# Another sharing table, a semaphore increment in every lot and small carrier instructions in a four-layer graph kernel on one core

## The chip, the cores and the metric

The kernel runs on one core of one Trainium2 chip. The metric is the device time of one execution in microseconds (us). The kernel before takes 5687.83 us, the median of three runs (5687.65 to 5688.55). The engines are named as the profile names them: PE (TensorE, with PEld for its weight loads), DVE (VectorE), ACT (ScalarE), POOL (GpSimd) and SP (SyncE, which only issues DMAs here).

## The reference

64 batches of 256 nodes with 128 features go through four layers, all in float32. Layer 0 is the costly one, because its leaky ReLU acts on every pair of nodes and each of 256 features.

```
def L0(x, W, b, a, bias):               # W = bias = adj, 256 x 256
    s1, s2 = x @ W[:, :F].T, x @ W[:, F:].T          # [B,K,256]
    pre = s1[:, :, None, :] + s2[:, None, :, :] + b  # [B,K,K,256]
    h = where(pre >= 0, pre, 0.2 * pre)
    attn = softmax(einsum('bije,e->bij', h, a) + bias)
    return sigmoid(attn @ x)
x = x + L0(relu(layernorm(x)), ...)
x = x + L1(relu(layernorm(x)), ...)   # elu, sigmoid edges times a mask, two dense layers
x = x + L2(relu(layernorm(x)), ...)   # masked attention, exp(8 tanh(QK/8/sqrt(d)))
x = x + L3(relu(layernorm(x)), ...)   # gated recurrent graph step, 5 times
```

## The kernel before

Batches are taken in pairs. The loop has 34 turns, which are written out one after the other for every engine (`run_turns`). Turn m computes the layer-0 scores of both batches of pair m (for m below 32), and beside them layers 1 and 2 of pair m-1 and layer 3 of pair m-2. Turns 0 and 1 lack a part of that, and turns 32 and 33 have only the later layers.

The layer-0 scores of a turn are cut into 128 lots, 64 for each batch of the pair. A lot is eight blocks. A block is one [128 features x 256 nodes] float32 tile `max(W, U[:, i])` (or the same through a ReLU) for one node i, written to one place of a ring with eight places. The eight blocks of every lot are shared among three engines by the table `SHARES`: the first ones go to DVE, the next to POOL and the last to ACT. DVE makes 1, 2, 4 or more neighbouring blocks with one instruction: 256 elements wide at L586, 512 or more at L591. POOL makes one block per instruction at L480, and ACT one per instruction at L779. When all three have signalled (`by_dve`, `by_pool`, `by_act`), PE multiplies the eight blocks with four 32-column matmuls (L980; the profile shows each as two matmuls and two weight loads, so a lot is 8 of them) and signals `freed`. An engine may write a place again only when the lot eight before it is freed.

The table comes from a planner, `share_blocks` (L111). It walks over the lots with one running time for each of the three engines. For every lot it takes the share whose latest end is smallest, at a fixed price per block and per lot: 2.67 per DVE block, 3.57 per ACT block, 4.5 per POOL block, and 1.0 for each lot on POOL (`POOL_START`). It adds what each engine does for the other layers in that lot (`stage_costs`). One planner unit stands for 0.1 us.

The other stages stand at fixed lots in every engine's stream (the tables `POST`, `PRE`, `LN1` to `L3`, counted in lots of a turn). An engine works its queue in order, so a stage that waits holds the blocks behind it. PE does the stages of lot t already behind lot t-3 (`LEAD`). At the turn's border these matter:

- lot 122: DVE adds the output of layer 3 (L735, `OUT`), which waits for PE's last transposes of that layer (L1127);
- lot 2: DVE computes the statistics for the norm of layer 3 (L638, then L644 `mv`), and POOL turns them into the norm's factors (L452 to L457) before its blocks of lot 3;
- lot 5: DVE reads the finished scores of the last batch (L620, `neg_score`);
- lot 10: DVE inverts the softmax sums (L625) and halves them (L628, `half_inv`, 2 elements wide).

Where a DVE stage needs the result that DVE itself just wrote, a ring piece is held back and put between (`one_piece`), to cover the latency.

Of the kernel before, what the change touches and what calls it, by code (L numbers as in the profile page):

```python
# [73 lines left out]
DVE_REST_TURNED, DVE_REST_ALL = 6, 7  # L74


VECTOR_BLOCK, VECTOR_START, SCALAR_BLOCK, POOL_BLOCK, POOL_START = 2.67, 0.69, 3.57, 4.5, 1.0
LARGEST = 3.4028234e38


# [98 lines left out]
def gnn_stack(nc, x, adj, L0_b, L0_a, L1_Wi, L1_bi, L1_We, L1_be, L1_Wn, L1_bn, L1_Wm, L1_bm, L2_q, L2_k, L2_v,  # L179
# [6 lines left out]
    class Turn:  # L186


        def __init__(self, m):
            self.m = m  # L190
            self.has_main = m < PAIRS
            self.has_post = [1 <= m <= PAIRS, self.has_main]
            self.has_l12 = 1 <= m <= PAIRS
            self.has_l3 = m >= 2
            self.pre_next = m < PAIRS - 1

        def at(self, per_turn, more):

            return per_turn * self.m + more

    def need(eng, sem, value):
        if value > 0:
            eng.wait_ge(sem, value)

    def run_turns(eng, body):
        for m in range(PAIRS + 2):
            body(Turn(m))

    with ExitStack() as ctx:
        def sb(name, shape):  # L210
# [54 lines left out]
        rstd0 = sb("rstd0", [P, NB])  # L265
        minus_mean0 = sb("minus_mean0", [P, NB])
        shift0 = sb("shift0", [P, NB])
        neg_score = sb("neg_score", [P, NB, N])
        prob = sb("prob", [P, NB, N])
        probT = sb("probT", [P, NB, N])  # L270
# [11 lines left out]
        X3_held = sb("X3_held", [P, 4, P])  # L282
        OUT = sb("OUT", [P, 4, P])
        st = sb("st", [P, 3, 4, 6])
        mv = sb("mv", [P, 3, 4, 2])
        var = sb("var", [P, 3, 4])
        rstd = sb("rstd", [P, 3, 4])
# [43 lines left out]
        by_dve = [sem(f"by_dve{n}") for n in range(RING)]  # L331
        by_act = [sem(f"by_act{n}") for n in range(RING)]
        by_pool = [sem(f"by_pool{n}") for n in range(RING)]
        freed = [sem(f"freed{n}") for n in range(RING)]

        x_loaded, pre_stats, pre_mv, pre_eps, pre_rstd = (sem(n) for n in "x_loaded pre_stats pre_mv pre_eps pre_rstd".split())
# [30 lines left out]
        def layer3_parts(turn, s):  # L367

            if turn.m <= PAIRS:
# [12 lines left out]
        @block.sync  # L385
        def _(sp):
            def load(dst, src, done=loaded_rest):
                sp.dma_start(dst, src, allow_slow_non_contiguous=True).then_inc(done, 16)


            sp.sem_inc(out_stored, 16)

            sp.dma_start(X0[:, 0], x_rows[0]).then_inc(x_loaded, 16)
            load(A[:], adj.rearrange("(r p) j -> p r j", p=P), loaded)
            load(a_col[:], L0_a.rearrange("(c p) -> p c", p=P), loaded)
            load(b0_col[:], L0_b.rearrange("(c p) -> p c", p=P), loaded)
            load(Wi[:], L1_Wi)
            load(We[:], L1_We.rearrange("(c p) o -> p (c o)", p=P))
            load(be[:], L1_be.partition_broadcast(P))
            load(Wn[:], L1_Wn.rearrange("(c p) o -> p c o", p=P))  # L400
            load(Wm[:], L1_Wm.rearrange("(c p) o -> p c o", p=P))
            load(bm_half[:], L1_bm.partition_broadcast(P))
            for n, b in enumerate((L1_bi, L1_bn, L3_w3_b, L3_w4_b, L3_w5_b, L3_u3_b, L3_u5_b)):
                load(cols[:, n:n + 1], b.rearrange("(p o) -> p o", o=1))
            load(raw2[:, 0], L2_q)
            load(raw2[:, 1], L2_k)
            load(Wv[:], L2_v)
            for n, w in enumerate((L3_w3_w, L3_w4_w, L3_w5_w)):
                load(raw3[:, n], w)
            load(rawu[:, 0], L3_u3_w)  # L410
            load(rawu[:, 1], L3_u5_w)

            def body(turn):
                for y in range(2):

                    if turn.has_main and (y == 0 or turn.pre_next):
                        need(sp, x1_ready, turn.at(2, y))
                        if turn.m == 0 and y == 0:

                            sp.wait_ge(pre_stats, 1)  # L420
                        b = turn.at(2, y + 1)
                        sp.dma_start(X0[:, 1 - y], x_rows[b]).then_inc(x_loaded, 16)
                if turn.has_l3:
                    sp.wait_ge(out_ready, turn.at(1, -1))
                    for y in range(2):
                        if turn.m == PAIRS + 1 and y == 1:

                            sp.wait_ge(out_ready, PAIRS + 1)
                        b = turn.at(2, y - 4)
                        sp.dma_start(out_rows[b], OUT[:, NB * y:NB * y + NB]).then_inc(out_stored, 16)  # L430
# [11 lines left out]
        def _(gp):  # L442
# [24 lines left out]
            def blocks(turn, t):  # L467
                y, p = divmod(t, LOTS_B)
                row, c = divmod(p, EC)
                place, rnd = t % RING, t // RING  # L470
                d, count, _ = SHARES[t]

                if p == 0:
                    gp.wait_ge(u_ready, turn.at(2, y + 1))
                    gp.wait_ge(w_ready, turn.at(2, y + 1))
                need(gp, freed[place], turn.at(ROUNDS, rnd))
                for n in range(d, d + count):
# [38 lines left out]
        def _(dve):  # L516
# [85 lines left out]
            def pre(p, y, value):  # L602

                if p == PRE[1 - y]["stats"]:
# [3 lines left out]
                    last.then_inc(pre_stats, 1)  # L608
                    one_piece()
                    dve.wait_ge(pre_stats, value)  # L610
                    for r in range(NB):
                        last = dve.bn_aggr(mv0[:, r], st0[:, r])
                    last.then_inc(pre_mv, 1)
            def post(p, y, value, lots_done):
                if p == POST[1 - y]["score"]:

                    dve.wait_ge(freed[RING - 1], lots_done)
                    need(dve, prob_ready, value - 1)
                    for r in range(NB):
                        last = dve.tensor_tensor_reduce(neg_score[:, r], S[y][:, r * N:(r + 1) * N], A[:, r], -1.0, LARGEST,  # L620
                                                        ALU.add, ALU.min, accum_out=neg_max[:, r:r + 1])
# [13 lines left out]
            def stats(t, ln, n, src, pair):  # L635
                if t == ln["stats"]:
# [3 lines left out]
                    one_piece()  # L640

                    dve.wait_ge(ln_stats[n], pair)
                    for r in range(4):
                        last = dve.bn_aggr(mv[:, n, r], st[:, n, r])  # L644
                    last.then_inc(ln_mv[n], 1)
# [536 lines left out]
```

## Time and profile before

| | us |
|---|---|
| median of three runs | 5687.83 |
| lowest and highest | 5687.65, 5688.55 |
| the profiled execution | 5687.65 |
| its span | 5685.0 |
| PE busy | 5607.0 (99%) |
| ACT busy | 5045.0 (89%) |
| DVE busy | 4978.0 (88%) |
| POOL busy | 4650.8 (82%) |

The span is the time from the first to the last instruction of the profile; the execution's own time is 2.65 us longer. PE's busy time counts matmuls from start to modelled end, and these overlap, so it can hide short stalls. The granted TensorE clock is full (2.4 GHz) through all the main turns. Times in the views are from the span's start.

### The profile page before, as it was taken

The numbers are of one execution on the slowest core, as the hardware profiler recorded it, in microseconds if no ns is written. First come the engines' busy times: TensorE is split into PE (matmuls) and PEld (weight loads), VectorE is DVE, ScalarE is ACT, GpSimd is POOL, SyncE is SP. The second block draws the span as 40 slices with busy tenths as digits, with TensorE's granted clock in tenths as the row PEclk, the third lists the DMA queues.
The fourth block names the chain that finished last, engine by engine and source line by source line (L and its number), as shares of the span: only waits on it lengthen the run. The fifth ranks groups of instructions, "written<-read, shape, count | busy, mean of one in ns | idle before, by whom it ended". The sixth has DMA issues, their size and how long they took to land.

```text
span 5685.0 us, 118726 instructions
## 1 busy us (share of the span) xinstructions
PE 5607.0 (99%) x40844; PEld 2178.3 (38%) x40844; DVE 4978.0 (88%) x8942; ACT 5045.0 (89%) x13145; POOL 4650.8 (82%) x9638
## 2 busy tenths in 40 slices
PE   8999999999999999999999999999999999999996
PEld 2333333333333333333333333333333333333334
DVE  9988988898988889888898888898898988889883
ACT  8999988899988989888998889998898988899883
POOL 8988888888888888888888888888888888888880
PEclk9999999999999999999999999999999999999999
DMA  0000000000000000000000000000000000000000
GB/s 14 5 3 6 7 7 6 3 6 7 7 6 3 7 6 7 6 3 7 6 7 7 6 3 6 7 7 6 3 7 6 7 6 3 7 6 7 7 5 6
DMA packets 44238, 34.15 MB, mean 6 GB/s; under 512 B 4736, under 2 KB 39552, under 8 KB 43648
## 3 DMA queue, kind: packets, MB, share of 16 engines
q1 hardware_dynamic: 43648, 26.56, 1.5%
q8 instruction: 336, 5.51, 0.4%
q14 instruction: 254, 2.08, 0.1%
HBM read 9.77 MB, written 8.39 MB: 3 GB/s over the span
## 4 chain that ended last, share of the span: by engine, by line
PE 83%; DVE 12%; ACT 3%; POOL 1%; issue 0%; DMA 0%; SPq 0%; POOLq 0%; DVEq 0%
PE S L980 51%; PE R L928 15%; DVE ring L591 8%; PE W L928 5%; PE S L928 4%; PE V L928 3%; PE R L1119 2%; ACT ring L779 2%; DVE ring L586 1%; PE R L1127 1%; POOL ring L480 1%; DVE half_inv L628 1%; PE S L972 1%; DVE st L638 0%; PE V L990 0%
## 5 line engine op out<-in xcount | busy, mean ns | idle before, releaser
L480 POOL TENSOR_SCALAR ring<-W,U 128x256 f32<-128x256 f32 x8928 | 4331.1, 503 | 361.1 <-PE S L980 342.7
L779 ACT ACTIVATE ring<-V,U_minus 128x256 f32<-128x256 f32 x10432 | 3969.3, 588 | 2.3 <-issue 1.1
L980 PE MATMUL S<-ring,a_window 128*32 128x512 f32 x32768 | 3699.4, 595 | 29.1 <-DVE ring L586 10.1
L591 DVE TENSOR_TENSOR ring<-U,W 128x512 f32<-128x512 f32 (+1 forms) x3840 | 3365.3, 905 | 50.4 <-ACT V L801 44.6
L980 PEld LDWEIGHTS S<-ring,a_window 128*32 128x32 f32 x32768 | 978.4, 109 | 2456.0 <-issue 2346.5
L586 DVE TENSOR_TENSOR ring<-U,W 128x256 f32<-128x256 f32 x2400 | 969.4, 408 | 0.0
L452 POOL TENSOR_TENSOR minus_mean<-mv,minus_one 128x4 f32<-128x4 f32 (+1 forms) x160 | 31.5, 197 | 571.5 <-DVE mv L644 476.4
L928 PE MATMUL R<-mT,W 128*128 128x512 f32 (+1 forms) x640 | 332.8, 602 | 2.1 <-ACT mT L887 2.1
L928 PE MATMUL R<-AT,h 128*128 128x256 f32 x1260 | 308.3, 388 | 2.8 <-ACT h L899 2.1
L717 DVE SCALAR_TENSOR_TENSOR rh<-tr,h3T 128x512 f32<-128x512 f32 (+1 forms) x165 | 123.1, 746 | 180.3 <-ACT tr L890 180.3
L887 ACT ACTIVATE mT<-R 128x512 f32<-128x512 f32 (+1 forms) x160 | 101.0, 632 | 196.5 <-PE R L928 195.0
L928 PEld LDWEIGHTS R<-AT,h 128*128 128x128 f32 x1260 | 228.9, 192 | 79.0 <-issue 50.3
L721 DVE TENSOR_TENSOR diff<-cand,h3T 128x512 f32<-128x512 f32 (+1 forms) x165 | 121.4, 736 | 134.5 <-ACT cand L896 134.5
L893 ACT ACTIVATE tz<-R,bias 128x512 f32<-128x512 f32 (+1 forms) x160 | 116.7, 729 | 75.9 <-PE R L1119 75.9
L928 PEld LDWEIGHTS R<-mT,W 128*128 128x128 f32 x640 | 111.8, 190 | 155.1 <-issue 149.6
L1119 PE MATMUL R<-mT,W 128*128 128x512 f32 (+1 forms) x320 | 165.3, 598 | 0.4 <-ACT tr L890 0.3
L928 PE MATMUL R<-rh,turned 128*128 128x512 f32 (+1 forms) x320 | 161.4, 586 | 0.2 <-DVE rh L717 0.2
L928 PE MATMUL R<-h3T,turned 128*128 128x512 f32 (+1 forms) x320 | 161.4, 586 | 0.0
L455 POOL TENSOR_TENSOR rstd<-var,minus_half 128x4 f32<-128x4 f32 (+1 forms) x160 | 142.7, 892 | 12.5
L673 DVE TENSOR_TENSOR selfT<-xhT,S 128x512 f32<-128x512 f32 x32 | 22.0, 686 | 131.6 <-PE S L928 131.6
L825 ACT ACTIVATE h<-X,shift,rstd 128x128 f32<-128x128 f32 x256 | 108.0, 531 | 32.3 <-POOL shift L457 32.3
L729 DVE SCALAR_TENSOR_TENSOR h3T<-gated,h3T 128x512 f32<-128x512 f32 (+1 forms) x165 | 126.1, 764 | 0.5
(172 smaller groups left out, 4107.9 us busy)
## 6 DMA issues: line engine op xcount, KB each, us to landing
X<-in_x SPq DMA_DIRECT2D x64, 128.0 KB, 2.1
X_held<-X SPq DMA_DIRECT2D x32, 256.0 KB, 2.3
out<-OUT SPq DMA_DIRECT2D x64, 128.0 KB, 1.9
raw<-in_L_gnn_w_w SPq DMA_DIRECT2D x3, 128.0 KB, 2.2
A<-in_adj SPq DMA_DIRECT2D x1, 256.0 KB, 2.6
Wn<-in_L_gnn_Wn SPq DMA_DIRECT2D x1, 128.0 KB, 2.5
Wm<-in_L_gnn_Wm SPq DMA_DIRECT2D x1, 128.0 KB, 2.4
rawu<-in_L_gnn_u_w SPq DMA_DIRECT2D x2, 64.0 KB, 2.2
```

Of the source, the lines that this page charges most:

```text
L455: gp.tensor_tensor(rstd_, eps_var, minus_half[:, 0:width], ALU.pow).then_inc(sem_rstd, 1)
L480: last = gp.tensor_scalar(ring[:, place, g, half * N:(half + 1) * N], W[:, y, c], LARGEST, U[:, y, c, i:i + 1], ALU.min, ALU.max)
L586: piece = dve.tensor_tensor(ring[:, place, g, half * N:(half + 1) * N], U[:, y, c, i:i + 1].to_broadcast([P, N]), w, ALU.max)
L591: piece = dve.tensor_tensor(ring[:, place, g:g + groups].rearrange("p g (h j) -> p g h j", h=NB), u.unsqueeze(3).to_broadcast([P, groups, ...
L717: dve.scalar_tensor_tensor(rh[:, cols_], tr[:, cols_], 1.0, h3T[:, cols_], ALU.add, ALU.mult).then_inc(rh_ready, 1)
L721: dve.tensor_tensor(diff[:, cols_], cand[:, cols_], h3T[:, cols_], ALU.subtract).then_inc(diff_ready, 1)
L729: dve.scalar_tensor_tensor(h3T[:, cols_], gated[:, cols_], 0.5, h3T[:, cols_], ALU.mult, ALU.add).then_inc(state_ready, 1)
L779: last = act.activation(ring[:, place, g, half * N:(half + 1) * N], W_scalar[y][:, c * N:(c + 1) * N], ACT.Relu, bias=U_minus[:, y, c, i:i ...
L893: act.activation(tz[:, cols_], gates[:, cols_], ACT.Tanh, bias=bias3[:, 0:1], scale=0.5).then_inc(tz_ready, 1)
L928: return pe.matmul(dst, lhsT, rhs, start=start, stop=stop)
L980: last = pe.matmul(S[y][g * ROWS:(g + 1) * ROWS, :], a_window[:, c, ROWS - 1 - row:2 * ROWS - 1 - row], ring[:, place, g], start=False, st ...
L1119: pe.matmul(gates[:, cols_], W345[:, 0], mT[:, cols_], start=False, stop=True, skip_group_check=True).then_inc(z_psum, 1)
```

## The change

`POOL_START` goes from 1.0 to 2.2, which gives another table `SHARES`. Summed over a turn the shares are 419 DVE, 279 POOL and 326 ACT blocks before, and 435, 253 and 336 after; 65 of the 128 lots have another share. DVE's pieces were 75 of one block, 68 of two and 52 of four. They are 69, 66 and 57, and one of six.

POOL increments a semaphore `pool_begun` at the start of every lot, between the wait for `freed` and the first block; nothing waits for it. DVE gets a memset of one element per partition (`wait_carrier` or `score_carrier`) behind the wait in three places: before the mean and variance are put together for layer 0 and for the norms of layers 1 to 3, and before the scores are read. `Turn` and its helpers learn a second form with a loop register `it`, but `run_turns` still makes every turn with m, so the code for that form produces nothing.

```
-VECTOR_BLOCK, VECTOR_START, SCALAR_BLOCK, POOL_BLOCK, POOL_START = 2.67, 0.69, 3.57, 4.5, 1.0
+VECTOR_BLOCK, VECTOR_START, SCALAR_BLOCK, POOL_BLOCK, POOL_START = 2.67, 0.69, 3.57, 4.5, 2.2
...
-            body(Turn(m))
+            body(Turn(m=m))
...
+        score_carrier = sb("score_carrier", [P, 1])
...
+        wait_carrier = sb("wait_carrier", [P, 1])
...
+        pool_begun = sem("pool_begun")
...
                 need(gp, freed[place], turn.at(ROUNDS, rnd))
+                gp.sem_inc(pool_begun, 1)
                 for n in range(d, d + count):
...
                     one_piece()
                     dve.wait_ge(pre_stats, value)
+                    dve.memset(wait_carrier[:], 0.0)
                     for r in range(NB):
                         last = dve.bn_aggr(mv0[:, r], st0[:, r])
...
                     need(dve, prob_ready, value - 1)
+                    dve.memset(score_carrier[:], 0.0)
                     for r in range(NB):
                         last = dve.tensor_tensor_reduce(neg_score[:, r], ...)
...
                     dve.wait_ge(ln_stats[n], pair)
+                    dve.memset(wait_carrier[:], 0.0)
                     for r in range(4):
                         last = dve.bn_aggr(mv[:, n, r], st[:, n, r])
```

DVE's queue before, from the output of layer 3 (lot 122) to the statistics of lot 2; `freedN` is the wait for the ring place of a lot, so freed6 is lot 126 and freed2 lot 2:

```order
L735 TENSOR_TENSOR OUT<-R,X_held 128x512 [waits out_stored,state_psum]
L591 TENSOR_TENSOR ring<-U,W 128x1024 [waits freed3]
L591 TENSOR_TENSOR ring<-U,W 128x512 [waits freed4]
L586 TENSOR_TENSOR ring<-U,W 128x256
L591 TENSOR_TENSOR ring<-U,W 128x1024 [waits freed5]
L591 TENSOR_TENSOR ring<-U,W 128x1024 [waits freed6]
L591 TENSOR_TENSOR ring<-U,W 128x1024 [waits freed7]
```

And the same piece of the queue now:

```order
L746 TENSOR_TENSOR OUT<-R,X_held 128x512 [waits out_stored,state_psum]
L599 TENSOR_TENSOR ring<-U,W 128x1024 [waits freed3]
L599 TENSOR_TENSOR ring<-U,W 128x512 [waits freed4]
L594 TENSOR_TENSOR ring<-U,W 128x256
L599 TENSOR_TENSOR ring<-U,W 128x1024 [waits freed5]
L599 TENSOR_TENSOR ring<-U,W 128x1024 [waits freed6]
L594 TENSOR_TENSOR ring<-U,W 128x256
L599 TENSOR_TENSOR ring<-U,W 128x1024 [waits freed7]
```

Lot 126 has one block more, an instruction of 256.

DVE's queue before from the statistics of lot 2 to lot 7:

```order
L638 BN_STATS st<-X_held 128x6 x3
L586 TENSOR_TENSOR ring<-U,W 128x256
L644 BN_AGGR mv<-st 128x2 [waits ln3_stats]
L644 BN_AGGR mv<-st 128x2 x3
L591 TENSOR_TENSOR ring<-U,W 128x512 [waits freed3]
L591 TENSOR_TENSOR ring<-U,W 128x1024 [waits freed4]
L591 TENSOR_TENSOR ring<-U,W 128x1024 [waits freed5]
L620 ISA neg_score,neg_max<-S,A 128x256 [waits prob_ready,freed7]
...
L591 TENSOR_TENSOR ring<-U,W 128x512 [waits freed6]
L591 TENSOR_TENSOR ring<-U,W 128x1024 [waits freed7]
L586 TENSOR_TENSOR ring<-U,W 128x256
```

And now:

```order
L648 BN_STATS st<-X_held 128x6 x3
L599 TENSOR_TENSOR ring<-U,W 128x512
L653 MEMSET wait_carrier 128x1 [waits ln3_stats]
L655 BN_AGGR mv<-st 128x2 x4
L599 TENSOR_TENSOR ring<-U,W 128x512 [waits freed3]
L599 TENSOR_TENSOR ring<-U,W 128x1024 [waits freed4]
L599 TENSOR_TENSOR ring<-U,W 128x512 [waits freed5]
L594 TENSOR_TENSOR ring<-U,W 128x256
L628 MEMSET score_carrier 128x1 [waits prob_ready,freed7]
...
L599 TENSOR_TENSOR ring<-U,W 128x1024 [waits freed6]
L599 TENSOR_TENSOR ring<-U,W 128x1024 [waits freed7]
```

The piece held back at lot 2 grows from one block to two, lot 5 goes from four blocks to three, lot 6 from two to four, lot 7 from five to four, and the two memsets carry the waits. DVE's queue from lot 8 to `half_inv` is unchanged.

POOL's queue before from the norm's factors to lot 8 (freed0):

```order
L457 TENSOR_TENSOR shift<-minus_mean,rstd 128x4 [waits ln3_rstd]
L480 TENSOR_SCALAR ring<-W,U 128x256 [waits freed3]
L480 TENSOR_SCALAR ring<-W,U 128x256 [waits freed4]
L480 TENSOR_SCALAR ring<-W,U 128x256 [waits freed5]
L480 TENSOR_SCALAR ring<-W,U 128x256 [waits freed6]
L480 TENSOR_SCALAR ring<-W,U 128x256 x3
L480 TENSOR_SCALAR ring<-W,U 128x256 [waits freed7]
L480 TENSOR_SCALAR ring<-W,U 128x256
L480 TENSOR_SCALAR ring<-W,U 128x256 [waits freed0]
L480 TENSOR_SCALAR ring<-W,U 128x256
```

And now (semaphore increments are not in these rows; one stands ahead of each row with a `freed` wait):

```order
L464 TENSOR_TENSOR shift<-minus_mean,rstd 128x4 [waits ln3_rstd]
L488 TENSOR_SCALAR ring<-W,U 128x256 [waits freed3]
L488 TENSOR_SCALAR ring<-W,U 128x256 [waits freed4]
L488 TENSOR_SCALAR ring<-W,U 128x256 [waits freed5]
L488 TENSOR_SCALAR ring<-W,U 128x256 [waits freed6]
L488 TENSOR_SCALAR ring<-W,U 128x256 x2
L488 TENSOR_SCALAR ring<-W,U 128x256 [waits freed7]
L488 TENSOR_SCALAR ring<-W,U 128x256 x2
L488 TENSOR_SCALAR ring<-W,U 128x256 [waits freed0]
```

Lot 6 has three blocks instead of four, lot 7 three instead of two, lot 8 one instead of two. Through lot 6 that is 6 blocks instead of 7, through lot 7 it is 9 as before.

## Rows read from the trace of the kernel before

**Rows 1.** Stretches turn 0, 1, 7: length, PE, PEld, DVE, ACT, POOL busy us, clock.

```profile
15.45:154.06 138.61, 130.19 (x1079) 36.55 (x1079) 135.70 (x230) 130.77 (x358) 131.05 (x291) 0.99 0.01 2
154.06:298.98 144.92, 141.69 (x1161) 49.35 (x1160) 137.33 (x257) 140.58 (x381) 136.72 (x298) 1.00 0.02 5
1174.19:1349.08 174.89, 174.44 (x1275) 67.46 (x1274) 155.35 (x279) 157.34 (x411) 145.84 (x301) 1.00 0.02 6
```

**Rows 2.** Chain of waits over a turn's border: start us, us, what.

```profile
1164.05 0.45 PE R L1127 x4
...
1164.52 0.69 DVE OUT L735
1165.21 1.73 DVE ring L591 x2
1166.94 0.33 DVE ring L586
...
1174.34 0.37 DVE mv L644 x4
...
1182.36 0.60 DVE ring L591
...
1183.35 1.52 DVE half_inv L628
...
1185.84 1.07 PE S L980 x8
```

**Rows 3.** The same chain, one turn later.

```profile
1339.42 0.69 DVE OUT L735
```

**Rows 4.** PE's weight loads in time, lots 2 to 11: start, us, what, [idle before].

```profile
1175.94 0.13 PEld L980 LDWEIGHTS S<-ring,a_window 128*32 128x32 f32 x4 [0.30 <-issue]
1177.09 0.19 PEld L980 LDWEIGHTS S<-ring,a_window 128*32 128x32 f32 x8 [1.02 <-issue]
...
1178.83 0.16 PEld L980 LDWEIGHTS S<-ring,a_window 128*32 128x32 f32 x4 [0.27 <-issue]
1179.81 0.19 PEld L980 LDWEIGHTS S<-ring,a_window 128*32 128x32 f32 x8 [0.81 <-issue]
1180.71 0.19 PEld L980 LDWEIGHTS S<-ring,a_window 128*32 128x32 f32 x8 [0.72 <-DVE ring L586]
...
1185.84 0.16 PEld L980 LDWEIGHTS S<-ring,a_window 128*32 128x32 f32 x8 [1.21 <-DVE ring L586]
```

**Rows 5.** POOL in order of time from the border, norm factors and lots 3 onwards.

```profile
1174.80 0.20 POOL L452 TENSOR_TENSOR minus_mean<-mv,minus_one 128x4 f32<-128x4 f32 x1 [3.95 <-DVE mv L644]
...
1176.50 10.89 POOL L480 TENSOR_SCALAR ring<-W,U 128x256 f32<-128x256 f32 x24
```

**Rows 6.** Chain of waits in turn 0, its two longest pieces.

```profile
68.61 11.66 ACT ring L779 x32
...
81.37 46.74 POOL ring L480 x103
```

**Rows 7.** Who waited for whom on POOL in turn 7: total, times, longest.

```profile
POOL minus_mean L452 <- DVE mv L644: 13.8, 3, 6.9
POOL ring L480 <- PE S L980: 11.2, 9, 3.6
```

**Rows 8.** One memset on DVE: minimum/median/maximum ns.

```profile
L739 DVE MEMSET minus_one<- x1: 62/62/62, 0.8 to 0.8; 128x4 f32 x1
```

**Rows 9.** POOL in order of time, norm factors of layer 1.

```profile
1195.74 1.02 POOL L455 TENSOR_TENSOR rstd<-var,minus_half 128x4 f32<-128x4 f32 x1
1196.83 0.20 POOL L457 TENSOR_TENSOR shift<-minus_mean,rstd 128x4 f32<-128x4 f32 x1
```

**Rows 10.** `half_inv` over the run: minimum/median/maximum ns.

```profile
L628 DVE TENSOR_SCALAR half_inv<-inv_sum x64: 156/164/1611, 96.2 to 5546.8; 128x2 f32<-128x2 f32 x64
```

**Rows 11.** DVE, then POOL, around one `half_inv` in order of time.

```profile
1183.27 1.60 DVE L628 TENSOR_SCALAR half_inv<-inv_sum 128x2 f32<-128x2 f32 x1
1181.92 4.11 POOL L480 TENSOR_SCALAR ring<-W,U 128x256 f32<-128x256 f32 x9
```

More of the change, by code:

```diff
@@ L74 @@
 DVE_REST_TURNED, DVE_REST_ALL = 6, 7
-VECTOR_BLOCK, VECTOR_START, SCALAR_BLOCK, POOL_BLOCK, POOL_START = 2.67, 0.69, 3.57, 4.5, 1.0
+VECTOR_BLOCK, VECTOR_START, SCALAR_BLOCK, POOL_BLOCK, POOL_START = 2.67, 0.69, 3.57, 4.5, 2.2
 LARGEST = 3.4028234e38
@@ L186, in gnn_stack, with __init__ @@
     class Turn:
[L189 to L195, printed above, removed]
+        def __init__(self, m=None, it=None):
+            self.m, self.it = m, it
+            self.has_main = it is not None or m < PAIRS
+            self.has_post = [it is not None or 1 <= m <= PAIRS, self.has_main]
+            self.has_l12 = it is not None or 1 <= m <= PAIRS
+            self.has_l3 = it is not None or m >= 2
+            self.pre_next = it is not None or m < PAIRS - 1
         def at(self, per_turn, more):
-            return per_turn * self.m + more
+            if self.it is None:
+                return per_turn * self.m + more
+            return self.it * per_turn + (2 * per_turn + more)
     def need(eng, sem, value):
-        if value > 0:
-            eng.wait_ge(sem, value)
+        if isinstance(value, int) and value <= 0:
+            return
+        eng.wait_ge(sem, value)
     def run_turns(eng, body):
         for m in range(PAIRS + 2):
-            body(Turn(m))
+            body(Turn(m=m))
     with ExitStack() as ctx:
@@ L267, in gnn_stack @@
         shift0 = sb("shift0", [P, NB])
+        score_carrier = sb("score_carrier", [P, 1])
         neg_score = sb("neg_score", [P, NB, N])
@@ L284, in gnn_stack @@
         st = sb("st", [P, 3, 4, 6])
+        wait_carrier = sb("wait_carrier", [P, 1])
         mv = sb("mv", [P, 3, 4, 2])
@@ L333, in gnn_stack @@
         by_pool = [sem(f"by_pool{n}") for n in range(RING)]
+        pool_begun = sem("pool_begun")
         freed = [sem(f"freed{n}") for n in range(RING)]
@@ L367, in layer3_parts @@
         def layer3_parts(turn, s):
-            if turn.m <= PAIRS:
+            if turn.it is not None or turn.m <= PAIRS:
                 return [(slice(0, 2 * N), slice(0, 2 * NB), R0, R1, turn.at(STEPS, s + 1 - 2 * STEPS),
@@ L421, in body @@
                         b = turn.at(2, y + 1)
-                        sp.dma_start(X0[:, 1 - y], x_rows[b]).then_inc(x_loaded, 16)
+                        sp.dma_start(X0[:, 1 - y], x_rows[b] if isinstance(b, int) else x_rows[bass.ds(b, 1)].rearrange("o p r d -> (o p) r d")).then_inc(x_loaded, 16)
                 if turn.has_l3:
@@ L429, in body @@
                         b = turn.at(2, y - 4)
-                        sp.dma_start(out_rows[b], OUT[:, NB * y:NB * y + NB]).then_inc(out_stored, 16)
+                        dst = out_rows[b] if isinstance(b, int) else out_rows[bass.ds(b, 1)].rearrange("o p r d -> (o p) r d")
+                        sp.dma_start(dst, OUT[:, NB * y:NB * y + NB]).then_inc(out_stored, 16)
                 if turn.has_l12:
@@ L476, in blocks @@
                 need(gp, freed[place], turn.at(ROUNDS, rnd))
+                gp.sem_inc(pool_begun, 1)
                 for n in range(d, d + count):
@@ L610, in pre @@
                     dve.wait_ge(pre_stats, value)
+                    dve.memset(wait_carrier[:], 0.0)
                     for r in range(NB):
@@ L618, in post @@
                     need(dve, prob_ready, value - 1)
+                    dve.memset(score_carrier[:], 0.0)
                     for r in range(NB):
@@ L642, in stats @@
                     dve.wait_ge(ln_stats[n], pair)
+                    dve.memset(wait_carrier[:], 0.0)
                     for r in range(4):
```

## The prediction

> **What bounds the kernel now.** I began with the busy times by stretch. In a full turn PE is busy for 174.44 of 174.89 us [rows 1], but that time counts to modelled ends, so I asked next for the chain of waits. From one turn's border to the next it is PE work without a break, except for one stretch: when PE has finished the last transposes of layer 3, DVE adds the output at 1164.52 and then runs 21.3 us without a pause, through the rest of the turn and into the next one, until its blocks of lot 11 let PE start that lot at 1185.84 [rows 2]. One turn later the same addition stands at 1339.42 [rows 3], so a turn takes 174.90 us. A turn is thus PE's work from lot 11 to lot 117, plus this DVE stretch.
>
> PE's weight loads show how much PE loses there [rows 4]. At full pace a load row and the idle ahead of it make 0.43 us (0.13 + 0.30, or 0.16 + 0.27) for half a lot. The idle ahead of lot 3 is 1.02 instead of 0.30, ahead of lot 6 it is 0.81 instead of 0.27, ahead of lot 11 it is 1.21 instead of 0.30: 0.72 + 0.54 + 0.91 = 2.17 us lost. Lot 7 comes 0.90 behind lot 6 where 0.86 is the pace, 0.04 lost. Who ends last? POOL waits for DVE's mv, makes the norm's factors and starts its blocks of lot 3 at 1176.50, then 24 without a gap at 10.89/24 = 0.454 each [rows 5]. Its first block ends near 1176.97, its seventh (the last of lot 6) near 1179.70 and its ninth (the last of lot 7) near 1180.60; PE starts lots 3, 6 and 7 each 0.11 to 0.12 us later. So these three wait for POOL, and lot 11 waits for DVE. About 2.2 us in 174.9 is all that a better sharing could win in a full turn.
>
> The two first turns are different: turn 0 (138.61 us) has DVE busy for 135.70, turn 1 (144.92 us) has ACT busy for 140.58 [rows 1], and a long piece of turn 0's chain is POOL [rows 6].
>
> **The change part by part.** Prices: a DVE piece of one block takes 0.33 us of the chain and one of two 0.60; a four and a two together take 1.73, so a four 1.13 [rows 2]. A POOL block takes 46.74/103 = 0.454 us and an ACT block 11.66/32 = 0.364 us [rows 6].
>
> Per turn the table takes 26 blocks off POOL (-11.8 us), gives ten to ACT (+3.6 us) and sixteen to DVE. In pieces DVE has six ones and two twos fewer, five fours more and one six (1.13 + 0.53 = 1.66, the step from two to four once more): -1.98 - 1.20 + 5.65 + 1.66 = +4.1 us. In a full turn most of this lies beside PE's work: of 174.89 us DVE is idle 19.5 and ACT 17.6 [rows 1]. POOL's relief is worth little there: POOL waits 11.2 us a turn for free ring places and 13.8 for DVE's mv as it is [rows 7].
>
> What counts is what falls into the DVE stretch. Lot 126: four blocks become five, +0.33. Lot 2: a held piece of one becomes one of two, +0.27. Lot 5: 1.13 becomes 0.60 + 0.33, -0.20. Lot 6: 0.60 becomes 1.13, +0.53. Lot 7: 1.13 + 0.33 becomes 1.13, -0.33. The sum is +0.60 us, all of it ahead of mv and 0 behind it.
>
> The memsets: the two in the stretch (lots 2 and 5) take 62 ns each from start to end [rows 8], and instructions overlap in that queue, so 0 to 0.06 us each. I take 0.03 each, +0.06. The others of a turn lie in covered places.
>
> The semaphore increment on POOL has no row of its own. From below: POOL's 24 blocks behind the border and its 103 in turn 0 follow at 0.454 us across lots, although each lot starts with a semaphore wait [rows 5, 6]; a semaphore operation whose condition is met costs this queue nothing, so the lower end is 0. From above: where POOL has to wait for the end of its own last instruction, the next starts 0.07 us behind it (1195.74 + 1.02 to 1196.83) instead of overlapping it by 0.02 [rows 9], so a full drain in each lot would be about 0.1 us. I take 0, the nearer row, and keep 0.1.
>
> The last term is a stall. `half_inv` handles 2 elements and takes 164 ns at the median, but up to 1611 [rows 10], and at the border it is the long form: 1.60 us [rows 11], 1.52 of them on the chain [rows 2]. In that time POOL ran on without a gap, nine blocks in 4.11 us [rows 11]: DVE was passed by three of them. That is 1.44 us for an unlucky moment. DVE comes to it over the same sum of pieces behind mv as before plus one memset, and POOL's grid of 0.454 us starts at mv too. So DVE comes about 0.03 us later against that grid. If it misses the unlucky moment, the wait is at most the rest of one block, 0 to 0.45 us, and 1.0 to 1.44 us are won; I take a wait of 0.3, 1.14 won. If it does not, nothing is won.
>
> The Trainium skill (SBUF — State Buffer, "Who interferes with whom") says of a DVE instruction in a two-port mode beside GpSimd: "Whoever issues first gets the shared pair for the whole instruction; the other **fully blocks**". The rows agree that DVE is held up while POOL runs, and disagree on how long: by the rule it would be one block, not three. By the rule alone at most 0.45 us could be won here, the border would change by 0.60 + 0.06 - 0.45 = +0.21, and the time would be 5696 us.
>
> Now the two paths to lot 11. DVE's end moves by +0.60 + 0.06 - 1.14 = -0.48 us. On PE's own path, mv and POOL's factors behind it come +0.63 later (0.60 and one memset). Through lot 7 POOL has nine blocks as before, so lot 7 starts +0.63 later, and from there PE has 0.91 us of stall to use up before lot 11: +0.63 - 0.91 = -0.28. The later of the two sets the turn, -0.28 us. What is late next is POOL at lots 3 to 7, not DVE. About 30 borders: -8.4 us.
>
> Turn 0: DVE's 135.70 + 4.1 + 7 x 0.03 = 140.0 is over the turn's 138.61, +1.4. Turn 1: ACT's 140.58 + 3.6 = 144.2 is just under 144.92; with imperfect packing I take +1 (-0.7 to +3.6). In the tail a few memsets stand on the chain, +0.1. Sum: -8.4 + 1.4 + 1.0 + 0.1 = -5.9. The profiled execution took 5687.65 us, 0.2 below the median, so 5681.8 against it and 5682 beside the median.
>
> **The rivals.**
>
> 1. *The stall stays.* DVE comes again just when POOL starts a block, since both count from mv and only a memset lies between. Then the whole +0.66 counts: 30 x 0.66 + 2.5 = +22.3, 5710 us. For it: the long form stands at the same place in a turn, so the phase is locked, and a shift of some ns may not leave it. Against it: half of the 64 `half_inv` are short although POOL is nearly always busy, so the window is narrow. It decides once the wait stays over some 0.8 us.
>
> 2. *The increment costs POOL 0.1 us a lot.* Five increments lie between mv and lot 7, +0.5: lot 11 at +0.22. 30 x 0.22 + 2.5 = +9.1, 5697 us. For it: nothing but that the price is not shown. The Trainium skill (PSUM — Partial Sum Buffer, "Engine vs sequencer instructions") counts semaphore operations as the sequencer's own, which waits only until earlier instructions are dispatched; by that the cost is 0, and no row here shows an increment of POOL's.
>
> 3. *POOL becomes the bound.* 128 increments must outweigh the 11.8 us taken off and the 11.2 us of waits for ring places, which they do from 0.18 us each. At 0.25 us it would be 32 - 23 = +9 us a turn, 5960 us. Nothing in the rows speaks for it.
>
> 4. *The relief pays where POOL is the chain.* In turn 0 some sixteen blocks leave the POOL-bound half, -7.2 us. If DVE and ACT take theirs in gaps, turns 0 and 1 get 3 us shorter each, and with -0.4 a border the sum is -18, 5670 us. Against it: DVE's busy time in turn 0.
>
> **How the numbers follow.** Forecast 0.45, rival 1 0.23, rival 2 0.14, rival 3 0.04, rival 4 0.14. A measurement of this kernel tells about 0.2% (11.4 us) from no change, so the borders are 5676.4 and 5699.2. Faster: rival 4 and a little of the forecast, 0.19. Same: most of the forecast and more than half of rival 2, 0.47. Slower: rivals 1 and 3 and the rest, 0.34. The range runs from rival 4 to rival 1 with its unknowns, 5669 to 5713; the forecast's own is 5674 to 5692.
>
> **What would show it.** A turn (one output addition to the next) should be 174.6 us. `half_inv` at the border should be under 0.65 us; if it is 1.6, rival 1 holds. PE should lose nearly nothing ahead of lot 11 and more ahead of lots 3 and 7. POOL's blocks should follow at 0.45 us across lots; a longer step is rival 2 or 3. DVE's output addition should still wait for PE. I am wrong if PE stalls elsewhere in the turn, at the updates of layer 3 (lots 29, 51, 73, 95, 117), where the added ACT and DVE blocks would then have used up the cover, or if a full turn changes by over 1 us either way.

## The result, and the profile after

The changed kernel takes 5739.15 us (median of six runs, 5728.78 to 5753.63) beside 5688.19 us for the kernel before (six runs, 5687.65 to 5688.97). The ratio is 1.009, with a 95% interval of 1.0077 to 1.0104. That is 51 us slower. The forecast was 5682 us and its range ended at 5713, so it was wrong, and not narrowly. The runs of the changed kernel also lie 25 us apart, where those of the kernel before lie 1.3 us apart. The profiled execution took 5721.63 us, less than any of the six timed ones. What it shows is therefore the lower end of the loss, and the rest has to be found by experiment. One run of the first experiment below took 11388 us, twice the time of its others, at a granted clock of 0.94, and is left out of its median.

The profile page, part 1 (busy us, share of the span, instructions): POOL's busy time fell as the table says, and DVE and ACT took it over.

```profile
PE 5615.9 (98%) x40844; PEld 2184.3 (38%) x40844; DVE 5103.7 (89%) x9102; ACT 5157.0 (90%) x13465; POOL 4247.0 (74%) x8806
```

Stretches of turn 0, turn 1 and turn 7, with the columns of [rows 1]:

```profile
15.47:155.22 139.75, 130.15 (x1078) 36.29 (x1078) 139.45 (x229) 134.21 (x369) 121.73 (x269) 0.99 0.01 2
155.22:303.19 147.97, 142.84 (x1161) 48.07 (x1160) 143.44 (x256) 144.33 (x391) 122.06 (x267) 1.00 0.02 5
1181.34:1356.84 175.50, 174.45 (x1278) 67.62 (x1274) 159.13 (x284) 160.85 (x421) 133.04 (x275) 1.00 0.02 6
```

Turn 0 lost 1.15 us, turn 1 lost 3.05, and an ordinary full turn 0.61. DVE is now busy for 139.45 of the 139.75 us of turn 0, but that counts time in which it is held up. Each batch ends with one DVE instruction that adds layer 0's output (`X<-tanh,X`, 256 elements). All executions of it, minimum/median/maximum ns, before and after:

```profile
L632 DVE SCALAR_TENSOR_TENSOR X<-tanh,X x64: 407/424/733, 104.0 to 5550.8; 128x256 f32<-128x256 f32 x64
L642 DVE SCALAR_TENSOR_TENSOR X<-tanh,X x64: 405/424/2442, 107.2 to 5581.9; 128x256 f32<-128x256 f32 x64
```

The long one stands in turn 1, while POOL runs without a gap (below: DVE, then POOL), and one of 1567 ns in turn 0 (733 before):

```profile
251.90 2.44 DVE L642 SCALAR_TENSOR_TENSOR X<-tanh,X 128x256 f32<-128x256 f32 x1
249.79 6.62 POOL L488 TENSOR_SCALAR ring<-W,U 128x256 f32<-128x256 f32 x14
```

The chain of waits over the same border (start us, us, what) answers to [rows 2, 3]:

```profile
1171.29 0.69 DVE OUT L746
...
1181.81 0.28 DVE mv L655 x3
...
1190.73 1.51 DVE half_inv L638
...
1193.22 1.07 PE S L991 x8
...
1346.79 0.69 DVE OUT L746
```

From the output addition to PE's start of lot 11 it is 21.93 us, against 21.32 before, and from one addition to the next 175.50. `half_inv` still holds the chain for 1.51 us.

PE's weight loads of lots 2 to 11 in order of time (start, us, what, idle before) answer to [rows 4]:

```profile
1184.46 0.19 PEld L991 LDWEIGHTS S<-ring,a_window 128*32 128x32 f32 x8 [1.63 <-issue]
...
1186.73 0.15 PEld L991 LDWEIGHTS S<-ring,a_window 128*32 128x32 f32 x4 [0.36 <-DVE ring L599]
1187.07 0.16 PEld L991 LDWEIGHTS S<-ring,a_window 128*32 128x32 f32 x4 [0.18 <-issue]
1188.09 0.19 PEld L991 LDWEIGHTS S<-ring,a_window 128*32 128x32 f32 x8 [0.86 <-DVE ring L599]
...
1193.22 0.16 PEld L991 LDWEIGHTS S<-ring,a_window 128*32 128x32 f32 x8 [1.21 <-DVE ring L594]
```

The idle ahead of lot 3 grew from 1.02 to 1.63 us, because mv and POOL's factors come 0.61 later. The rows of lots 6 and 7 (1186.73 and 1188.09) name DVE as the one that ended the idle time, but POOL's last block came later there: at 1187.97 for lot 7, against 1187.68 for DVE's. The idle ahead of lot 11 is 1.21 as before. Nothing was given back there.

POOL and DVE at that place, in order of time:

```profile
1183.88 11.33 POOL L488 TENSOR_SCALAR ring<-W,U 128x256 f32<-128x256 f32 x25
```

```profile
1190.65 1.59 DVE L638 TENSOR_SCALAR half_inv<-inv_sum 128x2 f32<-128x2 f32 x1
```

POOL's blocks follow at 11.33/25 = 0.453 us across some fourteen lots, with an increment in each: the increment costs POOL nothing.

What no row of before had shown are single long waits. `diff` is the first DVE instruction of each state update of layer 3 (five a turn; the first is due at lot 29). All executions of it in the trace, minimum/median/maximum ns, of the kernel after:

```profile
L732 DVE TENSOR_TENSOR diff<-cand,h3T x165: 416/693/4317, 336.5 to 5715.1; 128x512 f32<-128x512 f32 x155, 128x256 f32<-128x256 f32 x10
```

and of the kernel before:

```profile
L721 DVE TENSOR_TENSOR diff<-cand,h3T x165: 415/692/1018, 331.9 to 5680.2; 128x512 f32<-128x512 f32 x155, 128x256 f32<-128x256 f32 x10
```

The longest stands in turn 22. DVE, POOL and PE there, in order of time:

```profile
3847.09 4.32 DVE L732 TENSOR_TENSOR diff<-cand,h3T 128x512 f32<-128x512 f32 x1 [0.21 <-ACT cand L907]
3851.33 0.41 DVE L594 TENSOR_TENSOR ring<-U,W 128x256 f32<-128x256 f32 x1
```

```profile
3845.24 8.34 POOL L488 TENSOR_SCALAR ring<-W,U 128x256 f32<-128x256 f32 x15
```

```profile
3844.97 4.90 PE L991 MATMUL S<-ring,a_window 128*32 128x512 f32 x44
3852.75 1.08 PE L991 MATMUL S<-ring,a_window 128*32 128x512 f32 x4 [2.87 <-DVE ring L594]
```

DVE stands for 4.32 us over an instruction that needs 0.69 when nothing disturbs it, while POOL runs block after block. The next DVE block comes only then, and PE waits 2.87 us for it. The windows behind it show what follows (length, busy us of PE, PEld, DVE, ACT, POOL, granted clock, DMA share, GB/s):

```profile
3840.00:3852.00 12.00, 9.88 (x80) 3.01 (x72) 11.79 (x14) 12.00 (x33) 12.00 (x23) 1.00 0.01 2
3852.00:3859.00 7.00, 6.25 (x22) 1.99 (x26) 7.00 (x13) 4.45 (x12) 3.84 (x7) 0.51 0.00 0
```

PE had stood still for 2.87 us, and then the granted clock was 0.51, the lower level (1.2 GHz), for 7 us. This turn took 181.53 us (+6.03); turn 28, with a `diff` of 3890 ns and no drop of the clock, took 178.14 (+2.64).

So the 34.8 us between the two profiled spans (5685.0 and 5719.8) are: 28 ordinary turns at 0.605 = 16.9; the long waits of turns 22 and 28, and 0.25 in turn 20, 8.9; turns 0 and 1 4.2; the stretch from the last main turn's start to the end 4.6; 0.2 is left over. The term of 4.6 goes with the clock: from that start on, 40.2 us ran at the lower level in this trace, 30.9 before. Whether it is the change's own isn't settled. In the ten traces with new shares in all or part of the table the same stretch is 0.8 to 5.6 us longer than before, and roughly the longer, the more of it ran at the lower level (31.1 us for the 0.8, 43.7 for the 5.6). In the two further traces with the old table (increments and memsets alone, and no halving) it is 0.3 and 0.5 us shorter. One trace of each kernel can't tell more.

### The profile page after: what moved, and what is told of

Read it like the earlier page. It is cut to its first block, busy times and chain, and to the rows that moved or that the text cites. A ratio compares the mean times of both kernels' runs of the same rounds, so it can differ in the third digit from the quotient of the medians.

```text
span 5719.8 us, 122469 instructions
## 1 busy us (share of the span) xinstructions
PE 5615.9 (98%) x40844; PEld 2184.3 (38%) x40844; DVE 5103.7 (89%) x9102; ACT 5157.0 (90%) x13465; POOL 4247.0 (74%) x8806
## 3 DMA queue, kind: packets, MB, share of 16 engines
q14 instruction: 283, 2.32, 0.1%
## 4 chain that ended last, share of the span: by engine, by line
PE 82%; DVE 14%; ACT 2%; issue 1%; POOL 0%; DMA 0%; SPq 0%; POOLq 0%; DVEq 0%
PE S L991 50%; PE R L939 15%; DVE ring L599 10%; PE W L939 5%; PE S L939 4%; PE V L939 3%; PE R L1130 2%; DVE ring L594 2%; ACT ring L790 1%; PE R L1138 1%; DVE half_inv L638 1%; PE S L983 1%; DVE st L648 0%; PE V L1001 0%; DVE OUT L746 0%
## 5 line engine op out<-in xcount | busy, mean ns | idle before, releaser
L488 POOL TENSOR_SCALAR ring<-W,U 128x256 f32<-128x256 f32 x8096 | 3914.7, 503 | 575.0 <-PE S L991 530.7
L790 ACT ACTIVATE ring<-V,U_minus 128x256 f32<-128x256 f32 x10752 | 4100.5, 607 | 2.4 <-issue 1.2
L599 DVE TENSOR_TENSOR ring<-U,W 128x512 f32<-128x512 f32 (+1 forms) x3968 | 3555.4, 928 | 34.5 <-ACT V L812 28.8
L594 DVE TENSOR_TENSOR ring<-U,W 128x256 f32<-128x256 f32 x2208 | 894.0, 408 | 0.0
L901 ACT ACTIVATE tr<-R,bias 128x512 f32<-128x512 f32 (+1 forms) x160 | 116.5, 728 | 5.3 <-PE R L939 5.3
L907 ACT ACTIVATE cand<-R,bias 128x512 f32<-128x512 f32 (+1 forms) x160 | 118.7, 742 | 1.4 <-PE R L939 1.4
```

Of the source, the lines that this page charges most:

```text
L594: piece = dve.tensor_tensor(ring[:, place, g, half * N:(half + 1) * N], U[:, y, c, i:i + 1].to_broadcast([P, N]), w, ALU.max)
L599: piece = dve.tensor_tensor(ring[:, place, g:g + groups].rearrange("p g (h j) -> p g h j", h=NB), u.unsqueeze(3).to_broadcast([P, groups, ...
L790: last = act.activation(ring[:, place, g, half * N:(half + 1) * N], W_scalar[y][:, c * N:(c + 1) * N], ACT.Relu, bias=U_minus[:, y, c, i:i ...
L907: act.activation(cand[:, cols_], messages[:, cols_], ACT.Tanh, bias=bias3[:, 2:3]).then_inc(cand_ready, 1)
```

## Experiments

Two theories stood after this. S: the steady loss is DVE's added 0.60 us ahead of mv with the stall of `half_inv` unchanged, and the scatter is a second thing, long waits of DVE behind POOL at lot 29. R, the rival: the increments and memsets make the loss.

**The table alone.**

```
-                gp.sem_inc(pool_begun, 1)
-                    dve.memset(wait_carrier[:], 0.0)      (both)
-                    dve.memset(score_carrier[:], 0.0)
```

> The new sharing table alone: no increment on POOL, no memsets. Theory A (the table is the cause: +0.60 us of DVE blocks in the stretch at each turn's border with the long halving still in it, and new collisions of DVE with POOL's stream at lot 29): a turn of about 175.45 us, the halving at the border 1.6 us, the time 5715 to 5745 us and scattered by over 10 us. Theory B (the increment or the memsets cost the time, by slowing or shifting POOL): within 0.2% of before, 5680 to 5698 us.

Measured: 5711.55 us (three runs, 5710.93 to 5714.27), ratio 1.0043 [1.0026, 1.006]. Turns 140.13, 148.65, then 175.49 without exception. The longest `diff` took 998 ns. The table alone costs 24 us, steadily. In the profile (24.8 us) that is 28 turns at 0.60 = 16.8, turns 0 and 1 = 5.3, and 2.7 in the tail, where the clock varies. In turns 0 and 1 `X<-tanh,X` took 2004 and 2884 ns here: DVE's long waits in these two turns need neither increments nor memsets.

**The increments and memsets alone.**

```
-... POOL_START = 2.67, 0.69, 3.57, 4.5, 2.2
+... POOL_START = 2.67, 0.69, 3.57, 4.5, 1.0
```

> Increments on POOL and memsets on DVE with the sharing table of before. Theory A: 174.9 to 175.0 us a turn (two memsets of some 0.03 us at the border), 5687 to 5692 us, POOL's blocks still 0.45 us apart across lots. Theory B: most of the loss is here, 5715 us or more.

Measured: 5688.89 us (5687.33 to 5691.18, ten runs), ratio 1.0002 [0.9992, 1.0011], turns of 174.90. With the old table they cost nothing. R is refuted as it stands.

**No halving, in the kernel before and in the changed one.** ACT's copy of the probabilities halves them, and the tanh scales with `inv_sum`:

```
-  act.activation(probT[:], ..., ACT.Copy)
+  act.activation(probT[:], ..., ACT.Copy, scale=0.5)
...
-  dve.tensor_scalar(half_inv[:], inv_sum[:], 0.5, None, ALU.mult).then_inc(half_inv_ready, 1)
```

> The kernel before, but the halving of the inverse sums is folded into ACT's copy of the transposed weights (scale 0.5), so the DVE instruction that takes 1.6 us at the border is gone. If that wait is real time on the path: DVE reaches lot 11 1.5 us earlier, PE is then held by POOL at lots 3 to 7 as before and saves the 0.91 us ahead of lot 11: a turn of 174.0 us, 5658 to 5664 us. If the wait only stands in for one that the next DVE instruction would take over, or POOL's stream decides: 5685 us or more.

> The changed kernel without the halving. Theory A: the border loses the stall too, and PE is held by POOL at lots 3 to 7, which start 0.6 us later than before: 174.9 - 0.3 = 174.6 us a turn instead of 175.5, and the scatter stays if the waits of DVE at lot 29 stay, 5690 to 5720 us. If the loss of the change were not at the border, the halving's removal would give under 5 us against the changed kernel, 5730 us or more.

Measured on the kernel before: 5673.77 us (5671.78 to 5675.75), ratio 0.9974 [0.9964, 0.9983], turns of 174.38. Measured on the changed kernel: 5698.88 us (5696.06 to 5701.27), ratio to before 1.0019 [1.001, 1.0029], turns of 174.99. The whole stall is thus worth 0.51 us a turn, not 0.91. And between these two kernels, which have no stall to win or lose, the change still costs 174.99 - 174.38 = 0.61. The chain at the border of the first (start us, us, what) shows why there is nothing left to win:

```profile
1162.69 0.69 DVE OUT L733
...
1174.49 0.20 POOL shift L457
1174.69 0.46 POOL ring L480
...
1175.28 4.69 PE S L978 x40
```

The chain now leaves DVE at mv, goes over POOL's factors to lot 3, and PE runs on from there. Both paths, through lot 3 and through lot 11, contain the stretch from the output addition to mv, and that is where the +0.60 lies. In the changed kernel the removal brought 40 us on the median, far over 29 x 0.5: the scatter was gone too, and the longest `diff` took 1004 ns.

**The new shares only at the border, and only elsewhere.**

```
+SHARES = [NEW_SHARES[t] if t >= 122 or t <= 12 else OLD_SHARES[t] for t in range(LOTS)]
```

> The changed kernel with the new shares in lots 122 to 127 and 0 to 12 alone; in all other lots the old ones. Theory (the steady loss of 0.61 us a turn is DVE's 0.60 us more between the output addition and lot 11; the long waits of the state update at lot 29 and the loss in turns 0 and 1 come from the shares elsewhere): a full turn 175.5 us, no turn longer than 175.7, 30 x 0.6 = 18 on 5688, so 5704 to 5709 us, with a scatter of some 3 us between runs. Rival (the long waits come with the memsets and increments or with any longer turn): turns of 178 to 182 us here and there, 5715 to 5750 us with a scatter over 10 us.

> The changed kernel with the old shares in lots 122 to 127 and 0 to 12 and the new ones in lots 13 to 121. Theory (as above): a full turn 174.9 us apart from the turns with a long wait at lot 29, 2 to 6 us each; turn 0 and turn 1 longer by some 3 us together; 5692 to 5725 us with a scatter of over 5 us. Rival (the added DVE and ACT blocks of lots 13 to 28 cost nothing by themselves): 5688 to 5691 us without scatter.

Measured, border only: 5710.46 us (5709.04 to 5711.73), ratio 1.0039 [1.0024, 1.0054], full turns of 175.49 or 175.50 without exception, longest `diff` 1097 ns. Elsewhere only: 5709.36 us (5702.62 to 5718.09), ratio 1.0038 [1.0023, 1.0053], full turns of 174.90 except nine: 177.22, 179.14 and seven of 176.77, each with a `diff` of 3.4 to 3.9 us at lot 29. The loss has two separate halves in two separate places of the table, as S says. What S put down to the shares elsewhere alone, the loss of turns 0 and 1, comes from both: they lose +1.0 and +1.1 with the first, +0.7 and +1.7 with the second.

**A later `half_inv`.** A memset of 64, then of 512 elements of its own ahead of it:

```
                     dve.wait_ge(inv_ready, value)
+                    dve.memset(late[:], 0.0)
```

> The changed kernel with one memset of 64 elements of its own ahead of half_inv, so that DVE asks for it some 0.1 us later (a memset of one element takes 59 ns). Theory A (the long form is a matter of phase: DVE must ask while POOL starts a block): the wait falls to 0.45 us or less, and the turn to 175.0 to 175.2 us as when half_inv is gone (174.99), 5715 us or below. Theory B (whenever POOL streams without a gap, DVE is passed by three blocks there): half_inv stays at 1.5 to 1.7 us and the turn is 175.5 to 175.6 us.

> The changed kernel with a memset of 512 elements ahead of half_inv, so that DVE asks for it some 0.5 us later, one POOL block later. In the traces so far the wait ended at the 19th POOL block behind mv in nearly every turn, whether DVE asked at once or 0.08 us later. Theory C (something at that block of POOL's stream lets DVE in): half_inv shortens by what it comes later, to 1.0 to 1.2 us, the border stays at 21.9 us. Theory B (DVE is passed by three blocks wherever it asks): half_inv stays at 1.4 to 1.6 us, and the turn grows by some 0.5 us to 176.0.

Measured with 64 elements: 5738.29 us (5731.45 to 5747.75), ratio 1.0089 [1.0074, 1.0104]; ordinary turns 175.49, `half_inv` 1.52 us. With 512 elements, a single run: 5713.5 us, turns of 175.54. DVE at the border in that kernel:

```profile
1191.51 0.48 DVE L639 MEMSET late<- 128x512 f32 x1
1191.92 1.09 DVE L640 TENSOR_SCALAR half_inv<-inv_sum 128x2 f32<-128x2 f32 x1
1192.92 0.68 DVE L600 TENSOR_TENSOR ring<-U,W 128x512 f32<-128x512 f32 x1
```

Theory A, mine from the prediction, is refuted: DVE asked at two other moments and won nothing either time. Theory B (always three blocks) is refuted as well: the wait shrank by the 0.5 us that DVE came later, as theory C of the last expectation says. In the kernels before, after, table alone and both of these, `half_inv` ended 0.23 to 0.24 us into the 19th POOL block behind mv in nearly every turn. DVE's way out of the stall is thus fixed to POOL's stream, and POOL's stream is fixed to mv. Work put between mv and `half_inv` (at least up to 0.5 us) is nearly free (+0.05 us a turn for 512 elements), work put ahead of mv is paid in full. Why it is that block isn't settled.

**Which part brings the long waits at lot 29.** The new table with the increments but no memsets, then with the memsets but no increments:

```
-                    dve.memset(wait_carrier[:], 0.0)      (first kernel, all three memsets)
-                gp.sem_inc(pool_begun, 1)                 (second kernel)
```

> The changed kernel without the memsets: new table and increments. With the table alone the runs stood at 5713 us without scatter; with all three parts at 5729 to 5754 us. Theory I (the increment at the head of each lot of POOL's shifts POOL against DVE and lets the long waits of the state update at lot 29 appear): 5725 to 5750 us, scatter over 10 us, single turns of 178 to 182 us. Theory M (the memsets shift DVE against POOL): 5711 to 5715 us, every full turn 175.5 us.

> The changed kernel without the increments: new table and memsets. Theory M: 5725 to 5750 us, scatter over 10 us, single turns of 178 to 182 us. Theory I: 5711 to 5716 us, every full turn 175.5 us. If both this kernel and the one without memsets scatter, each shift alone is enough; if neither does, it takes both.

Measured without memsets: 5711.13 us (5707.68 to 5714.37), ratio 1.0041 [1.0026, 1.0056], turns of 175.49, longest `diff` 993 ns. Without increments: 5716.79 us (5712.91 to 5734.98), ratio 1.0057 [1.0041, 1.0074], two turns of 178.13 with a `diff` of 3878 ns. One of them, in turn 3:

```profile
512.78 3.88 DVE L731 TENSOR_TENSOR diff<-cand,h3T 128x512 f32<-128x512 f32 x1 [0.21 <-ACT cand L906]
```

So the memsets are what lets the waits at lot 29 in, given the new table. Which of the three memsets does it wasn't tried. With the increments on top the median is 22 us higher still (5739 and 5717), so these seem to make the waits more frequent, though alone they bring none. This second point is weaker than the first: it rests on four runs and seven, one of the four stands at 5734.98 among the seven, and both profiles have two long waits.

**The old shares in lots 13 to 29 alone.**

```
+SHARES = [NEW_SHARES[t] if not 13 <= t <= 29 else OLD_SHARES[t] for t in range(LOTS)]
```

> The changed kernel with the old shares in lots 13 to 29 alone. There the new table gives DVE one block more and ACT two more and POOL three less; DVE's blocks of lot 29 are ready 0.05 us ahead of PE with it (1.16 us in the kernel before). Theory (the long waits and the scatter come from those lots): a full turn 175.5 us with no long wait of the state update at lot 29, 5705 to 5714 us, scatter of 5 us or less. Rival (they come with the sharing behind lot 29, which sets how long POOL streams without a gap): long waits remain, 5720 to 5750 us.

Measured: 5708.98 us (5706.72 to 5709.67, five runs), ratio 1.0035 [1.0021, 1.0049]; turns of 175.50, longest `diff` 982 ns. Memsets and increments are in, the shares of 111 lots are new, and the scatter is down to 3 us. Seventeen lots decide it.

What these lots change is when DVE asks. I took the start of `diff` at lot 29 in every full turn and the start of POOL's block in hand:

| kernel | `diff` starts so far into POOL's block | and takes |
|---|---|---|
| before | 321 to 328 ns | about 706 ns |
| increments and memsets alone | 307 to 330 | about 701 |
| border only | 303 to 377 | about 697; 1097 (at 377) |
| old shares in lots 13 to 29 | 317 to 337 | about 695 |
| lighter border, no halving (below) | 211 to 222 | about 797 |
| table alone | 21 to 47 | 990, at most 998 |
| table and increments | 21 to 44 | 984, at most 993 |
| changed, no halving | 5 to 35 | 1000, at most 1004 |
| before, no halving | 26 to 56 | 976, at most 990 |
| changed, 512 elements ahead of `half_inv` | 0 to 19, once 452 | 1009, at most 1019 |
| table and memsets | 19 to 47 | 992; twice 3878 (both at 47) |
| changed | 18 to 46 | 990; 3890 (at 29), 4317 (at 46) |
| changed, 64 elements ahead of `half_inv` | 14 to 46 | 994; six times 3878 to 3886 (at 19, 28 and four times 46) |
| new shares but at the border | 15 to 37 | 991; 3885 (at 23), 3881 (at 32), eight times 3439 (at 16 or 17) |

At 0.32 us into a block DVE isn't held up, at 0.21 it is by 0.1 us. Within the first 0.05 us it always waits for the rest of that block (990 ns), and sometimes for six to eight blocks, the one in hand included. All twenty long waits of `diff` in these traces came within 16 to 47 ns of a block's start. An early request is thus what these lots bring, but not enough by itself: five kernels with it had no long wait in their profiles. What picks the turn stays open; in the changed kernel two executions at the same 46 ns, in turns 22 and 23, went both ways. No run moved the request at lot 29 by itself, with the shares left as they are.

**A lighter border.** On the kernel before, without halving:

```
+for _t, _s in ((124, (2, 3, 3)), (126, (3, 4, 1)), (127, (2, 4, 2)), (0, (2, 3, 3)), (1, (2, 4, 2))):
+    SHARES[_t] = _s
```

> The kernel before, without half_inv (ACT's copy of the probabilities halves them) and with other shares in five lots ahead of mv (DVE, POOL, ACT): lot 124 (3,2,3) to (2,3,3), 126 (4,3,1) to (3,4,1), 127 and 1 (4,2,2) to (2,4,2), 0 (3,2,3) to (2,3,3). DVE gets 0.33 + 0.20 + 0.53 + 0.33 + 0.53 = 1.9 us less ahead of mv, POOL seven blocks = 3.2 us more where it waits 3.95 us for mv [rows 5]. Theory (DVE's stretch ahead of mv sets the turn, POOL's wait there is free): the turn falls from 174.4 (half_inv removed alone) by up to what PE still loses at lots 3 to 11, to 172.9 to 173.6 us, and the time to 5625 to 5650 us. Rival (POOL comes late to mv or to lot 3, or DVE's move shifts it against POOL into a long wait elsewhere): the turn stays at 174.4 or rises, 5674 us or more.

Measured: 5660.15 us (5658.69 to 5660.52), ratio 0.995 [0.9934, 0.9967]; turns of 173.84. The mechanism is as expected, the size isn't: the turn was to be 172.9 to 173.6. I had summed the idle of PE's weight loads at lots 3 to 7 (0.72 + 0.54 + 0.04) and got 0.54, and turns 0 and 1 gave nothing (+0.5 and +0.1). The chain at the border (start us, us, what):

```profile
1160.40 0.44 PE R L1127 x4
1160.83 8.72 PE S L980 x80
1169.55 1.06 PE S L972 x2
1170.61 7.00 PE S L980 x64
1177.61 0.59 PE V L1007 x4
```

DVE is gone from it. PE runs through the border, and this is the fastest of all versions, 28 us below the kernel before. The time missed the expected 5625 to 5650 us.

## Why the prediction was wrong

**Step by step.** *The two paths at the border*: right. OUT to lot 11 through DVE, and mv to lot 3 through POOL. *The table adds 0.60 us ahead of mv*: right; the stretch grew by 0.61, and so did the turn in each pair of kernels that differ in the border's shares alone. *Memsets 0.03 each in the stretch*: too much; with the old table the turn went from 174.89 to 174.90. *The increment costs POOL nothing*: right, and rival 2 is out. POOL's pace is 0.453 us, and the kernel with increments and memsets on the old table stands at 1.0002. *Rival 3*: out by POOL's pace. *Rival 4*: out; turns 0 and 1 became longer, not shorter.

**The step that failed** is the stall: "DVE comes about 0.03 us later against that grid. If it misses the unlucky moment, the wait is at most the rest of one block ... I take a wait of 0.3, 1.14 won." The wait isn't a matter of a moment. It ends at a fixed block of POOL's stream, wherever DVE asks within half a microsecond, and the trace of before already had the hint: the long form stood at 1.60 us at the same place in every full turn, to within some ns. A chance event doesn't repeat to 1%. Rival 1 said this, and its turn (+0.66) was the right one; measured was +0.61. I gave it 0.23 and should have made it the forecast.

**A second error in the same step** would have spoiled the forecast even so. I took PE's 0.91 us of idle weight loads ahead of lot 11 as time to be won. With the stall gone altogether, the turn fell by 0.51, and in the changed kernel it was 174.99, still 0.10 longer than before, where the forecast had it 0.28 shorter. PE's matmuls in the kernel before, in order of time, would have warned me:

```profile
1182.76 2.78 PE L980 MATMUL S<-ring,a_window 128*32 128x512 f32 x24
1185.84 1.07 PE L980 MATMUL S<-ring,a_window 128*32 128x512 f32 x8 [0.30 <-DVE ring L586]
```

They were idle for 0.30 us ahead of that lot by their modelled ends. The loads run ahead of the matmuls, and part of their idle is covered by matmuls still under way. So the idle of the loads is an upper bound, and the modelled idle of the matmuls a lower one.

**What wasn't in the sum** is the larger half. Rival 1's number was 5710, and five kernels with the new border and no long waits stand at 5709 to 5713 (border only, old shares at lots 13 to 29, table alone, with increments, and the profiled run of after less its 8.9 us of long waits, 5712.7). That rival 1's number is met so closely is partly luck, as it has 2.5 us for turns 0 and 1 and the tail, where the table alone lost 8. The remaining 26 us of the median I put down to long waits at lot 29, without traces of the timed runs. By the profiled ones, 2.6 us each without a drop of the clock, that would be about ten in 30 turns, an estimate. The profiled run with 64 elements ahead of `half_inv`, which took 5731.45 us with six of them, fits it. I had named the place: "I am wrong if PE stalls elsewhere in the turn, at the updates of layer 3 (lots 29, ...), where the added ACT and DVE blocks would then have used up the cover". The cover fell from 1.16 us (DVE's last block of lot 29 ready ahead of PE) to 0.05. But I gave it no term and no share of the range. The cover was only part of it: a wait 2.9 us over the usual one cost 2.64 us with 0.05 of cover and 2.32 with 0.25 (new shares but at the border), so the old 1.16 would have absorbed under half by these two figures, an estimate. The larger part is the wait itself. The rows had both parts of it: DVE held up behind POOL in one place, and in lots 13 to 29 a table that adds one DVE block and two ACT blocks.

**Turns 0 and 1.** I had +1.4 and +1.0; measured were +1.15 and +3.05. The number for turn 0 is near by luck in part. In the kernels with the whole new table turn 0 lost 0.5 and 0.6 us where its `X<-tanh,X` took 970 and 1039 ns, and 1.15 to 1.6 where it took 1567 to 2005, so a wait of DVE goes with half or more of the loss, and the sum had no term for it. For turn 1 I had written -0.7 to +3.6 and taken +1; its loss is 3.0 to 4.0 us in these kernels, with and without such a wait, and what makes it stays open.

**Of the three parts of the change**, then: the table costs 24 us by itself, increments and memsets together nothing without the table, the increments nothing with it, and the memsets some 28 us on top of the table and the increments (5739.15 against 5711.13). One-at-a-time trials would not have found the last.

## What to carry to other kernels

Ask of a stall what ends it, not only what begins it: if its end is tied to another engine's stream, work ahead of the common start is paid in full, work inside the stall is free, and only removing the stall wins. Where DVE and POOL hold each other up, look also at how far into POOL's block DVE asks, before and after an edit. An edit that costs nothing by itself can show up as scatter, so compare the spread of the runs as well as the median. Take the idle of the weight loads for an upper bound of what PE loses.

## What the runs showed of the hardware

A DVE instruction behind a gap-free POOL stream (blocks 0.453 us apart) waited for the rest of one block (990 instead of 690 ns) in most turns at lot 29, for three blocks at `half_inv` in nearly every turn (1.59 us), and for six (3.44 us), seven (3.88, 3.89) or eight (4.32) at lot 29 in some. The Trainium skill (SBUF — State Buffer, "Who interferes with whom") has the loser wait until the holder's instruction is finished. The rows agree that it is held up and agree on the usual wait at lot 29, but in the other cases POOL's next blocks went first.

A PE pause of 2.87 us in the middle of full work was followed by 7 us at 0.51 of the clock; the other long wait of that trace left the clock at 1.00. That makes one such wait cost 6.0 us and the other 2.6. Of the twenty long waits of `diff` in all traces four were followed by a drop: this one, and three with 3.4 us at the lower level, which made the turn 4.2 to 4.3 us longer.
